# Attention block with a time-mixing feed-forward on one core: scalings of the mixes on GpSimd, v copied by one instruction, and the residual input loaded at the head of a step

## What is computed

```python
h = x @ W1 + b1                                   # q, k, v of 16 heads, 8 features each
w = einsum('bhqd,bhkd->bhqk', q, k) / sqrt(8)     # causal mask, softmax
a = einsum('bhqk,bhkd->bhqd', softmax(w), v)
x = layernorm(x + a @ Wp + bp)
x_prev = x shifted by one token, zero for the first
xr = mu_r * x + (1 - mu_r) * x_prev
xk = mu_k * x + (1 - mu_k) * x_prev
out = sigmoid(xr @ W_r.T) * (square(relu(xk @ W_k.T)) @ W_v.T)
x = layernorm(x + out)
```

## Time and profile before

| | us |
|---|---|
| median of 3 runs | 726.02 |
| lowest and highest | 722.94, 727.3 |
| the profiled execution, as timed | 729.24 |
| its span in the profile | 727.5 |
| PE busy in the span | 612.0 (84%) |
| DVE busy | 553.3 (76%) |
| ACT busy | 470.4 (65%) |
| POOL busy | 368.2 (51%) |

### The profile page before, as it was taken

How to read it: one execution, slowest core, us unless ns; L and a number is a source line. 1 busy time by engine, 2 the same in 40 slices (tenths; PEclk the granted TensorE clock), 3 DMA queues, 4 the chain that set the end, 5 groups by cost and what they waited for, 6 DMA issues and landing times.

```text
span 727.5 us, 17681 instructions
## 1 busy us (share of the span) xinstructions
PE 612.0 (84%) x6729; PEld 275.7 (38%) x6729; DVE 553.3 (76%) x1654; ACT 470.4 (65%) x917; POOL 368.2 (51%) x518
## 2 busy tenths in 40 slices
PE   4468887898989989898989889898989898897873
PEld 2122333344343435343443434343443434342342
DVE  1476785779888787979788887979797887875327
ACT  2104773776868676777868676767768686767741
POOL 3002333455555556555646555565545565555643
PEclk9999997999999999999999999999999999999976
DMA  4752525142443636242634535342525435300011
GB/s 142 112 133 45 148 46 161 25 139 50 104 119 61 161 61 163 51 140 44 158 56 89 134 61 160 62 145 59 143 41 119 105 66 142 61 18 17 17 30 30
DMA packets 72203, 65.80 MB, mean 90 GB/s; under 512 B 9333, under 2 KB 63926, under 8 KB 72118
## 3 DMA queue, kind: packets, MB, share of 16 engines
q1 hardware_dynamic: 71410, 64.41, 37.5%
q10 hardware_dynamic: 708, 0.26, 0.2%
HBM read 34.70 MB, written 29.88 MB: 89 GB/s over the span
## 4 chain that ended last, share of the span: by engine, by line
PE 55%; DVE 20%; ACT 8%; issue 7%; POOL 4%; DMA 4%; ACTq 1%; SPq 1%; POOLq 0%; DVEq 0%
PE ops L623 15%; DVE rowmax L851 12%; PE sps L596 10%; PE tps L558 9%; PE spare L482 7%; ACT probs L764 6%; PE spare L502 4%; PE sps L581 3%; DVE h L902 3%; POOL probs L1029 2%; DMA xres<-L_attn_x 2%; PE spare L534 2%; PE spare L518 1%; DVE y L890 1%; PE spare L497 1%
## 5 line engine op out<-in xcount | busy, mean ns | idle before, releaser
L851 DVE TENSOR_REDUCE rowmax<-sps 128x1 f32<-128x512 f32 (+7 forms) x1024 | 401.3, 448 | 100.1 <-PE sps L596 99.4
L764 ACT ACTIVATE probs<-tps 128x512 f32<-128x512 f32 x640 | 346.4, 595 | 147.9 <-PE tps L558 147.9
L1029 POOL TENSOR_SCALAR_AFFINE_SELECT probs<-probs 128x512 f32<-128x512 f32 x256 | 158.8, 638 | 259.5 <-ACT probs L764 259.4
L623 PE MATMUL ops<-probs,vop 128*32 128x384 f32 (+3 forms) x2048 | 174.8, 449 | 7.1 <-POOL probs L1029 5.8
L558 PE MATMUL tps<-qop,kop 50*128 50x384 bf16 (+3 forms) x1024 | 126.9, 306 | 40.2 <-ACT probs L764 36.4
L596 PE MATMUL sps<-kop,qop 48*64 48x512 bf16 (+7 forms) x2048 | 130.4, 310 | 7.3 <-DMA kop<-d_parts 7.3
L581 PE MATMUL sps<-qmask,dup 64*128 64x128 bf16 (+1 forms) x640 | 69.7, 214 | 33.3 <-DVE rowmax L851 29.0
L558 PEld LDWEIGHTS tps<-qop,kop 50*128 50x128 bf16 x1024 | 34.2, 94 | 161.7 <-ACT probs L764 115.1
L623 PEld LDWEIGHTS ops<-probs,vop 128*32 128x32 f32 x2048 | 50.9, 110 | 82.2 <-issue 62.2
L596 PEld LDWEIGHTS sps<-kop,qop 48*64 48x64 bf16 x2048 | 43.1, 106 | 49.5 <-issue 19.3
L581 PEld LDWEIGHTS sps<-qmask,dup 64*128 64x128 bf16 x640 | 31.4, 95 | 75.6 <-DVE rowmax L851 69.3
(11 more groups left out here) (123 smaller groups left out, 585.0 us busy)
## 6 DMA issues: line engine op xcount, KB each, us to landing
qop<-d_parts SPq DMA_DIRECT2D x64, 192.0 KB, 4.3
kop<-d_parts SPq DMA_DIRECT2D x63, 192.0 KB, 4.8
d_parts<-qk_parts SPq DMA_DIRECT2D x15, 768.0 KB, 3.7
d_parts<-qk_parts SPq DMA_DIRECT2D x15, 512.0 KB, 4.9
d_parts<-qk_parts SPq DMA_DIRECT2D x17, 256.0 KB, 5.5
xa<-L_attn_x SPq DMA_DIRECT2D x16, 256.0 KB, 3.0
xres<-L_attn_x SPq DMA_DIRECT2D x16, 256.0 KB, 3.3
out<-result SPq DMA_DIRECT2D x15, 256.0 KB, 2.7
```

The lines of the kernel that those rows point to most:

```text
L623: last = nc.tensor.matmul(ops[32 * t:32 * t + 32, BLK * a:SEQ], vop[:, par, a, QUARTET * half + t, hh, :], probs[:, g % 2, i, off:off + w] ...
L764: nc.scalar.activation(probs[:, g % 2, i, :], tps[:, bank(n), :], ACT.Exp, scale=SCALE)\
L851: last = nc.vector.reduce_max(rowmax[:, par, QUARTET * half + i, a:a + 1], sps[:, bank(n), off:off + w], axis=AX_X)
L1029: last = nc.gpsimd.affine_select(out=v, in_=v, compare_op=ALU.is_ge, fill=0.0, base=0, pattern=[[0, QUARTET], [1, BLK]], channel_multiplie ...
```

## The change

Three edits. The scalings of the mixes go from ACT to POOL: `scale_steps` is gone, and `mix_sum` now makes one mix at a time, with a `tensor_scalar` by a column of `mus` and the addition. The one for the key is made ahead of `mask_group` of group 0, the one for the gate ahead of that of group 1. `scaled` is one tile instead of two. The copy of v is one instruction with the same places as destination. And the load of `xres` is the first thing that SP does in a step.

```diff
 [sync engine, step(b)]
+                if active("D", b):
+                    wait(sp, xbias_done, before("D", b))
+                    sp.dma_start(xres[:], x[b + OFFSET["D"]].rearrange("(t p) e -> p t e", p=P)).then_inc(xres_in, 16)
                 if active("S", b):
...
-                if active("D", b):
-                    wait(sp, xbias_done, before("D", b))
-                    sp.dma_start(xres[:], x[b + OFFSET["D"]].rearrange("(t p) e -> p t e", p=P)).then_inc(xres_in, 16)
 [tensor engine, spare_use]
                 elif use == "key":
-                    wait(pe, mixed_done, 2 * n + 2)
+                    wait(pe, mixed_done, 2 * n + 1)
                     last = nc.tensor.matmul(spare[:], wffT[:, 1, :], mixed[:, 1, :], start=True, stop=True)
                 elif use == "gate":
+                    wait(pe, mixed_done, 2 * n + 2)
 [scalar engine]
-                    for hh in range(2):
-                        ins = nc.scalar.copy(vop[:, par, :, :, hh, DH * hh:DH * hh + DH],
-                                             spare[:].rearrange("k (t p h d) -> k h t p d", t=TT, p=PAIRS, h=2)[:, hh])
+                    places = vop[:, par].rearrange("k t p h (c d) -> k (t p) (h c) d", d=DH)
+                    ins = nc.scalar.copy(places[:, :, 0:6:5, :],
+                                         spare[:].rearrange("k (a h d) -> k a h d", h=2, d=DH))
...
-            def scale_steps(n):
-                wait(act, step_done, n + 1)
-                wait(act, mixed_done, 2 * n)
-                for i in range(2):
-                    nc.scalar.activation(scaled[:, i, :], step_d[:], ACT.Copy, scale=mus[:, i:i + 1])\
-                        .then_inc(scaled_done, 1)
...
-                    if tg == 9 and active("D", tb) and before("D", tb) < LAST:
-                        scale_steps(before("D", tb))
 [GpSimd]
-            def mix_sum(n):
-                for i in range(2):
-                    wait(pool, scaled_done, 2 * n + i + 1)
-                    nc.gpsimd.tensor_tensor(mixed[:, i, :], scaled[:, i, :], hT[:, 0:SEQ], ALU.add)\
-                        .then_inc(mixed_done, 1)
+            def mix_sum(n, i):
+                wait(pool, step_done if i == 1 else mixed_done, n + 1 if i == 1 else 2 * n + 1)
+                nc.gpsimd.tensor_scalar(scaled[:], step_d[:], mus[:, i:i + 1], None, ALU.mult).then_inc(scaled_done, 1)
+                wait(pool, scaled_done, 2 * n + 2 - i)
+                nc.gpsimd.tensor_tensor(mixed[:, i, :], scaled[:], hT[:, 0:SEQ], ALU.add).then_inc(mixed_done, 1)
...
-                    if tg == 0 and active("E", tb) and before("E", tb) < LAST:
-                        mix_sum(before("E", tb))
+                    if tg in (0, 1) and active("E", tb) and before("E", tb) < LAST:
+                        mix_sum(before("E", tb), 1 - tg)
```

More of the change, by code:

```diff
@@ L236, in block_program @@
         step_d = sb("step_d", [P, SEQ])
-        scaled = sb("scaled", [P, 2, SEQ])
+        scaled = sb("scaled", [P, SEQ])
         mixed = sb("mixed", [P, 2, SEQ])
```

## The result

| | before | changed |
|---|---|---|
| median, us | 726.11 | 716.89 |
| lowest to highest of 4 runs, us | 722.94 to 727.3 | 714.15 to 717.75 |
| profiled execution: as timed, span, us | 729.24, 727.5 | 717.75, 716.0 |
| ratio of the times, 95% interval | | 0.9873 (0.9832 to 0.9914) |

The changed kernel is faster by 1.3%, by 9.2 us in the medians and by 11.5 us in the two profiled spans. The forecast was 711.7 us with a range of 706 to 719: the direction is right and the range holds the time, but the forecast gain of 14.3 us was 2.5 to 5 us too large.

A forecast was written before the change was run, and what follows sets the result against it. No engine is full; PE waits 0.92 us per step for ACT's scalings and 3.78 us once for a mask behind xres, then at half clock. 5.9 + 7.9 + 0.5 = 14.3 us off the 726.02 median gives 711.7, range 706 to 719.

The forecast's parts named there:

- clock falls anyway: Rival: PE's clock drops in step 1 despite the early load, which gains 3.8 instead of 7.9; 715.8 us, chance 0.08.
- gap filled: Rival: in groups 0 and 1 DVE's maxima set the pace, only xres pays; 717.6 us, chance 0.14.
- the likeliest case: The forecast itself, 711.7 us with its own range of about 709 to 715; chance 0.64.
- Scalings off ACT: Group 0: exponentials start 0.54 us earlier, DVE's first maximum limits PE's gain to 0.42 at 14 places, 5.9 us.
- a guess of 0.04: Group 0: time for the signal from DVE's first maximum to the mask matmuls of S, 0.04 us.
- The 40.28 of the prediction: Sign in the profile after: a step of about 39.8 us instead of 40.28, taken over eight steps.
- the one that gives PE its whole wait back: Rival: group 0 regains PE's whole 0.92 us wait, 12.9 instead of 5.9 us; 704.7 us, chance 0.07.
- get in each other's way: Rival: POOL's scalings stretch DVE's maxima, losing 0.42 us a step; counted within the filled-gap chance of 0.14.
- Scalings onto POOL: Groups 0 and 1: each scaling 0.6 us, between 0.29 and 1.25, hidden under the exponentials; cost 0.
- The room of 2.9 us: POOL ahead of group 1's mask: one scaling may take up to 2.9 us before that mask is late for PE.
- The load of xres: Step 1: early load removes PE's 3.78 us wait and the half clock behind it, 7.9 us; other steps 0.5.
- the split of the maxima: Queued behind the scalings on POOL in the usual step, needed later than 311.7; no cost.

The follow-up runs named there:

- e4: The changed kernel with each scaling done twice on POOL, one after the other: median 734.77 us, ratio to before 1.0105.
- e3: The changed kernel with all scalings left out, each mix being step_d plus the shifted tokens: median 715.71 us, ratio to before 0.9838.
- e1: The kernel before with only the scalings moved to POOL: median 726.25 us, ratio to before 1.0014.
- e8: The kernel before with only the copy of v made one instruction: median 726.28 us, ratio to before 0.9991.
- e12: The kernel before with the scalings on POOL and the load of xres first on SP in step 15 only: median 720.43 us, ratio to before 0.9903.
- e9: The changed kernel measured again, nothing altered: median 715.42 us, ratio to before 0.9837.
- e2: The kernel before with only the load of xres moved to the head of each step: median 719.27 us, ratio to before 0.9913.
- e11: The kernel before with the load of xres at the head in step 1 only: median 719.86 us, ratio to before 0.9899.
- e7: The changed kernel with the number 0.5 instead of the column of mus in POOL's scalings: 714.47 us in one run.

## Why the prediction was right, and where its sum was off

The time alone would not tell the forecast from two of its rivals: 716.89 lies nearer to 715.8 (clock falls anyway) and 717.6 (gap filled) than to 711.7, and outside the 709 to 715 of the likeliest case. The wide range held it. It is the traces that put both rivals out, since the steps are shorter and the clock stays at 1.00.

**Scalings off ACT: right mechanism, 0.42 us should be 0.36.** PE's second pair came 0.55 earlier against its first (0.54 had been worked out), and DVE's first maximum then held back the mask matmuls of S, as worked out. The mask matmuls start 1.54 us behind the first pair and DVE's maxima 0.79, so the first maximum and its signal take 0.75; I had half of 1.29 and a guess of 0.04, that is 0.69. The step is 40.16 - 39.80 = 0.36 shorter. (The 40.28 of the prediction is a mean over eight steps, three of them longer than usual; the usual step was 40.16.) The first rival (another wait fills the gap) is out, and so is the one that gives PE its whole wait back. POOL and DVE did not get in each other's way either: the maxima beside a scaling took 0.65 us each (2.61 for four at 256.26), as before (1.29 for two).

**Scalings onto POOL: the price was wrong, the conclusion held but for one step.** 1.57 us lies above both the value of 0.6 and the bound of 1.25. The bound failed because I took an instruction with one input to be no dearer than one with two. The room of 2.9 us (e4: about 2.85) covers it in steps 2 to 14. In step 15, which has no maxima to reduce and is shorter, the same room isn't there; there the forecast gain of 0.42 became 0.16: "13 to 15" gained 0.52 in all, of which 0.36 belong to the step of 14. The scalings thus gave 13 x 0.36 + 0.16 = 4.8 us instead of 5.9.

The Trainium skill, GPSIMD Engine Reference, sections 3 and 4.1, from which I had 769 ns as the best case for 512 elements, says in its table that a one-input operation is roughly at line rate. The row of L1053 disagrees with the table: 1573 ns, twice the best case. Its advice to keep elementwise work off GpSimd held in step 15 (0.43 us) and did not matter elsewhere (e3).

**The load of xres: the step that was mis-sized.** The sum had 7.9 us, read from one execution, and took it from the median of others. The stall of 3.78 us is there in three of four profiles (3.78 to 4.00), but the half clock behind it cost 1.4 to 1.8 us in the other three and not 4.2. Against a step 1 without stall (38.02, or 37.67 with the scalings off ACT), the four profiles that have it lose:

| profile | step 1 to 2 loses | of it PE's wait | the rest |
|---|---|---|---|
| before | 7.98 | 3.78 | 4.20 |
| e1 | 5.77 | 4.00 | 1.77 |
| e8 | 5.44 | 3.90 | 1.54 |
| e12 | 3.29 | 1.87 | 1.42 |

The rest goes with the time at the lower granted clock behind the stall: 9.6 us before, 3.9 in e1, 3.4 in e8 and e12, so each of these microseconds cost 0.42 to 0.45 us. In e12 the lower level lasts only from about 118 to 121.5 (before first, then e12, PE and its clock alone):

```profile
125.00:128.00 3.00, 3.00 (x20) 0.50 0.15 17
```

```profile
119.00:122.00 3.00, 3.00 (x20) 0.59 0.62 131
122.00:125.00 3.00, 2.98 (x43) 1.00 0.96 131
```

So the execution that I read was 3.2 us above the median in part because of this very stretch, and I subtracted the price of the bad case from the time of the usual one. Against its own time the sum gave 714.9, and the changed kernel's profiled execution took 717.75; of the 2.8 us between them, 1.1 are the scalings above, and 1.7 lie in the stretches ahead of the q projection of step 1 and behind `y` of step 15 (99.8 and 44.2 us before, 100.4 and 45.2 changed), which differ as much between the changed kernel and e9, the same kernel (101.1 and 42.2). With 5.4 to 5.8 us for the load (e1 and e8) and 4.8 for the scalings, the sum is 10.2 to 10.6, and the two measurements of the changed kernel gave 9.2 and 11.8. That the median execution lies there is read from three profiles beside that of before; the timed runs, 6.7 us in e2 and 7.4 in e11, each give or take about 2, agree with it but would not exclude 7.9.

**What no rival named.** That the two edits depend on each other: alone the scalings bring nothing in time (e1), since in step 15 they delay the exchange of the maxima and with it a load that stands behind it on SP. The prediction named the split of the maxima as queued behind the scalings on POOL, but looked at it in the usual step alone, where it comes late enough; it did not look at step 15, nor at what waits behind that exchange on SP. In the changed kernel the load has left that queue place, so this could not show.

## What to carry to other kernels

A duration read from one profiled execution may be that execution's own: before subtracting a stall and a fallen clock from a median, see how the profiled time stands to it, and price the stall and the clock apart. When work is put on an engine in its idle time, work out the room at the narrowest step of the pipeline and not only at the usual one, and follow what the engine feeds into in-order queues. The room is worth more than the price: here the price was wrong by a factor of 2.6 and the reading of the room, within 0.1 us, saved the forecast in all steps but one.

## What the runs showed of the hardware

A `tensor_scalar` of 128x512 float32 on GpSimd takes 1.57 us with a column and 1.51 with a number (e7), where the addition of two such tiles takes 1.27 and ScalarE's scaling 0.72. The one of 32x128 elements at 0.29 us, with another type of result, was no measure for it: four times its length took more than five times as long.

With an idle time of 1.87 to 4.00 us on PE in step 1 the granted clock fell to its lower level in all four profiles, in e1 within the idle time, in e12 about 1 us after PE had gone on. It stayed there from 3.4 us to 10 us, also at stalls of nearly the same length (3.90 and 3.78 us). In e1 and e11 it also fell once with waits of no more than 0.53 us ahead of it. What decides it was not tested.
